# Row maxima of 112 pairs of key blocks found as s0 + relu(s1 - s0) in the attention stage of a two-layer block

## The reference, cut to what matters

```
q = _apply_rope(q, cos, sin)
k = _apply_rope(k, cos, sin)
att = jnp.einsum('bhtd,bhsd->bhts', q, k) * scale
att = jnp.where(causal_mask[None, None], -jnp.inf, att)
att = jax.nn.softmax(att, axis=-1)
o = jnp.einsum('bhts,bhsd->bhtd', att, v)
```

## Time and profile before

| | us |
|---|---|
| median of 3 runs (1504.44 to 1509.45) | 1509.25 |
| the profiled execution, its own time | 1505.93 |
| its span, first to last instruction | 1504.2 |
| busy in the span: PE, DVE, ACT, POOL | 1316.1, 1276.6, 998.6, 321.6 |

### The profile page before, as it was taken

One profiled execution on the slowest core, in us unless ns is written; L12 is line 12 of the kernel. 1 busy time (PEld: TensorE's weight loads), 2 busy tenths in 40 slices (PEclk: granted clock), 3 DMA queues, 4 the chain that ended last, 5 costly groups with the idle time before them and its releaser, 6 DMA issues. The chain is left out here.

```text
span 1504.2 us, 27425 instructions
## 1 busy us (share of the span) xinstructions
PE 1316.1 (87%) x9558; PEld 597.4 (40%) x9558; DVE 1276.6 (85%) x2276; ACT 998.6 (66%) x1316; POOL 321.6 (21%) x574
## 2 busy tenths in 40 slices
PE   4786999999999999999999986999767767889987
PEld 2444223232232332323322212766533334467754
DVE  6896899999999999999999942799878999765668
ACT  3452365888888888888888896665357666356642
POOL 3220000110102111020110202333100077300475
PEclk9887688999999999999999998999968888899999
DMA  6887402141423304242043024596354155686776
GB/s 204 277 261 211 63 28 45 22 81 27 83 46 42 84 7 78 46 79 49 6 78 77 12 49 116 158 317 208 123 192 141 37 176 178 226 260 208 229 228 196
DMA packets 158521, 186.16 MB, mean 124 GB/s; under 512 B 18228, under 2 KB 134708, under 8 KB 157364
## 3 DMA queue, kind: packets, MB, share of 16 engines
q1 hardware_dynamic: 135384, 151.45, 37.5%
q0 software_dynamic: 6144, 16.79, 3.6%
q10 hardware_dynamic: 16864, 16.26, 3.1%
HBM read 100.81 MB, written 83.36 MB: 122 GB/s over the span
## 5 line engine op out<-in xcount | busy, mean ns | idle before, releaser
L1333 DVE TENSOR_REDUCE att_m_part<-att_mx 128x1 f32<-128x512 f32 (+3 forms) x1152 | 680.6, 653 | 30.3 <-PE att_mx L1401 13.5
L1363 ACT ACTIVATE att_prob<-att_score,late_score_scale 128x1024 f32<-128x1024 f32 (+3 forms) x640 | 594.9, 987 | 166.3 <-PE att_score L1440 164.1
L1401 PE MATMUL att_mx<-early_kop,early_qop 48*128 48x512 f16 (+3 forms) x1280 | 354.9, 367 | 23.0 <-DVE att_neg_m L1312 6.1
L1423 PE MATMUL att_pv<-att_prob,early_v 128*32 128x512 f32 (+3 forms) x2560 | 304.1, 547 | 2.1 <-POOL att_prob L1300 2.0
L1440 PE MATMUL att_score<-early_qop,early_kop 50*128 50x512 f16 (+3 forms) x1280 | 252.9, 356 | 11.1 <-ACT att_prob L1363 10.1
L1401 PEld LDWEIGHTS att_mx<-early_kop,early_qop 48*128 48x128 f16 x1280 | 98.5, 94 | 374.1 <-DVE att_m_part L1333 346.3
L1300 POOL TENSOR_SCALAR_AFFINE_SELECT att_prob<-att_prob 128x256 f32<-128x256 f32 x256 | 102.7, 406 | 669.7 <-ACT att_prob L1363 668.9
L2231 PE MATMUL rwkv_prod<-rwkv_xm,late_mixT 128*128 128x512 f32 x192 | 99.2, 672 | 34.5 <-ACT rwkv_kvr L2185 25.6
L1440 PEld LDWEIGHTS att_score<-early_qop,early_kop 50*128 50x128 f16 x1280 | 72.1, 94 | 71.7 <-ACT att_prob L1363 55.9
L2453 POOL DMA_INDIRECT moe_yg<-results,routing_slot_i x64 | 65.0, 1016 | 125.4 <-issue 124.3
L1980 POOL DMA_INDIRECT rows<-rwkv_xs,routing_slot_i x64 | 66.7, 1042 | 115.6 <-DVE routing_slot_i L2072 96.4
(11 more groups left out here) (263 smaller groups left out, 1759.7 us busy)
## 6 DMA issues: line engine op xcount, KB each, us to landing
va<-qkv_v SPq DMA_DIRECT2D x8, 1024.0 KB, 6.4
early_v<-va SPq DMA_DIRECT2D x8, 1024.0 KB, 6.8
routing_xp<-parts SPq DMA_DIRECT2D x32, 256.0 KB, 3.6
moe_xt<-rows SPq DMA_DIRECT2D x30, 256.0 KB, 3.2
rows<-att_zeros SPq DMA_DIRECT2D x8, 928.0 KB, 6.5
early_kop<-qk SPq DMA_DIRECT2D x48, 128.0 KB, 4.5
results<-moe_y ACTq DMA_DIRECT2D x24, 256.0 KB, 2.8
results<-blend_x ACTq DMA_DIRECT2D x22, 256.0 KB, 3.1
```

What stands on the lines that cost most here:

```text
L1333: nc.vector.tensor_reduce(cells[:, sides[0]:sides[-1] + 1, some], mx[:, banks[0]:banks[-1] + 1, 0:len(hps) * w].rearrange("p a (h w) -> p ...
L1363: nc.scalar.activation(prob[:, r % (PROBS * HP), :, n0:], score[:, r % 2, :, n0:], ACT.Exp, scale=late_weights.score_scale[:, 0:1])\
L1401: op = nc.tensor.matmul(bank[:, n * w:(n + 1) * w], qop[rows, slot, t, hp, i * P:(i + 1) * P], kop[rows, slot, hp, c * GT:c * GT + w], sta ...
L1423: op = nc.tensor.matmul(pv[at, n0:], v[:, slot, j, at], prob[:, (st * HP + h // 2) % (PROBS * HP), h % 2, n0:], start=(j == 0), stop=(j == ...
```

## The change

For 7 blocks of maxima, (iteration 0, t = 2) and (iterations 0 to 5, t = 3), the key blocks 0 and 1 are no longer two pieces. For each tile of 128 queries and head pair (8 in a block, 56 in all, each with two sides, so 112 pairs) the program now does this:

- POOL writes once for an iteration `k_minus` = -k for keys 0 to 511, in two instructions of 48x1024 f16 (L1337).
- PE computes s1 - s0 for both sides into a score bank: four matmuls of 512 columns in place of the two of key block 1 (`differences`, L1492).
- ACT takes the Relu of the 1024 columns into `over`, a ring of OVERS = 7 in SBUF (`overs`, L1432).
- PE computes s0 into an `att_mx` bank, as before, and DVE adds the two and takes the row maximum with `tensor_tensor_reduce` (L1389), in place of two `tensor_reduce`.

The score banks are now numbered by the place in the joint list of Relus and exponentials. The order of the pieces within a paired block changes (by tile and head pair, then key block), and `matrix_order` gets a fourth kind of work, "over", and other costs.

```diff
+    PAIRED = [(0, LATE - 1)] + [(it, LATE) for it in range(NIT - 2)]
+    OVERS, AHEAD = 7, 60
...
+        if in_pairs:
+            rest = [(i, (hp,), c) for i in range(TG) for hp in range(HP) for c in (0, *range(2, t + 1))
+                    if c < t or HP * width(t, i, t) > GT]
...
-        hand, back, mask, row, copy, soon = 250, 120, 420, 6500, 580, 200
-        turn = {"max": 0, "score": 1, "value": 2}
+        hand, back, mask, row, copy, soon, load = 250, 120, 420, 6500, 580, 200, 9000
+        turn = {"max": 0, "over": 1, "score": 2, "value": 3}
...
+                if it > 1:
+                    need.append(value_end[(it - 1) * NS - 1] + load if len(value_end) >= (it - 1) * NS else None)
+                if None not in need and (not paired(it, e) or pair_of[it, e] < done["over"]):
+                    ready.append((max(need) + back, "max"))
+            n = done["over"]
+            if n < total["over"] and done["max"] > max(pair_at[n] - AHEAD, place[0, ("turn", 0)]) and (n < OVERS or done["max"] > pair_end[n - OVERS]) \
+                    and done["score"] >= ((pairs[n][0] - 1) * NS + last_step[LATE - 1] + 1) * HP:
+                ready.append((max([0] + exp_end[-2:-1]) + back, "over"))
...
-                    dve = max(dve, pe + hand) + 70 + size * len(e[5]) * 100 // 96
+                    dve = max(dve, pe + hand) + 118 + size * len(e[5]) * 100 // 96
...
+            if kind == "over":
+                pe = when + 20 + GT * 5 // 6
+                start = max([act, pe + hand] + ([taken[pair_end[n - OVERS]] + hand] if n >= OVERS else []))
+                act = start + 894
...
-                act = start + 30 + columns(t, j) * 2 * 100 // 96
+                act = start + 380 + columns(t, j) * 2 * 593 // 1000
...
-                pe = when + 150 + columns(t, j) * 5 // 3
+                pe = when + 20 + columns(t, j) * 5 // 3
...
+        over = s.sb("over", [P, OVERS, 2, GT])
+        k_minus = s.sb("k_minus", [P, 2, HP, GT], F16)
...
+            def minus(it):
+                slot = it % 2
+                pool.wait_ge(first_in[slot], (it // 2 + 1) * FIRST)
+                if it > 1:
+                    last_pair = max(n for n, at in enumerate(pairs) if at[0] == it - 2)
+                    pool.wait_ge(score_done.sem, score_done.done(ring["over", last_pair]))
+                for a in range(2):
+                    rows = slice(HALF * a, HALF * a + ROWS)
+                    nc.gpsimd.tensor_scalar(k_minus[rows, slot], kop[rows, slot, :, 0:GT], -1.0, None, ALU.mult)\
+                        .then_inc(k_turned, 1)
+                    pool.wait_ge(k_turned, it * 2 + a + 1)
...
+                if paired(it, e):
+                    n, a = pair_of[it, e], sides[0]
+                    dve.wait_ge(exp_done.sem, exp_done.done(ring["over", n]))
+                    nc.vector.tensor_tensor_reduce(over[:, n % OVERS, a], mx[:, banks[0], 0:w], over[:, n % OVERS, a], 1.0,
+                                                   LOWEST, ALU.add, ALU.max, cells[:, a, some]).then_inc(m_found, 1)
+                    return
...
+            def overs(n):
+                at = ring["over", n]
+                if n >= OVERS:
+                    act.wait_ge(m_found, pair_end[n - OVERS] + 1)
+                act.wait_ge(score_done.sem, score_done.done(at))
+                nc.scalar.activation(over[:, n % OVERS], score[:, at % 2], ACT.Relu).then_inc(exp_done.sem, 1)
...
+            def differences(n):
+                it, t, i, (hp,) = pairs[n]
+                slot, at = it % 2, ring["over", n]
+                if n == 0 or pairs[n - 1][0] < it:
+                    pe.wait_ge(first_in[slot], (it // 2 + 1) * FIRST)
+                    pe.wait_ge(k_turned, it * 2 + 2)
+                    if it == 0:
+                        pe.wait_ge(att_in.third_in, att_in.THIRD)
+                pe.wait_ge(exp_done.sem, exp_done.freed(at, 2))
+                for step, moving in enumerate((kop[:, slot, hp, GT:2 * GT], k_minus[:, slot, hp])):
+                    for a in range(2):
+                        rows = slice(HALF * a, HALF * a + ROWS)
+                        op = nc.tensor.matmul(score[:, at % 2, a], qop[rows, slot, t, hp, i * P:(i + 1) * P], moving[rows],
+                                              start=step == 0, stop=step == 1)
+                op.then_inc(score_done.sem, 1)
```

More of the change, by code:

```diff
@@ new lines, in chunks, with paired, with_turn @@
+        return [("max", t, *item, (a,)) for item in whole + rest for a in range(2)]
+    def paired(it, e):
+        return e[0] == "max" and e[4] == 0 and (it, e[1]) in PAIRED
+    def with_turn(it, t):
+        own = [(it, e) for e in chunks(t, (it, t) in PAIRED)]
+        return own[:6] + [(it, ("turn", t - 1)) if t else (it - 1, ("turn", LATE))] + own[6:]
+    order_of = [(it, t) for it in range(NIT) for t in range(QB)]
+    entries = [at for n, (it, t) in enumerate(order_of) for at in with_turn(it, t) if at[0] >= 0]
@@ new lines, in attention_phase @@
+    entries.append((NIT - 1, ("turn", LATE)))
+    place = {entry: k for k, entry in enumerate(entries)}
+    pairs = []
+    for it, e in entries:
+        if paired(it, e) and (it, *e[1:4]) not in pairs:
+            pairs.append((it, *e[1:4]))
+    pair_of = {(it, e): pairs.index((it, *e[1:4])) for it, e in entries if paired(it, e)}
+    pair_at = [place[it, ("max", t, i, hps, 0, (0,))] for it, t, i, hps in pairs]
+    pair_end = [place[it, ("max", t, i, hps, 0, (1,))] for it, t, i, hps in pairs]
@@ L1105, in matrix_order @@
         exp_end, prob_end, value_end, out_end, found, rows = [], [], [], [], {}, {}
-        bank_end, order, done = [0] * BANKS, [], {"max": 0, "score": 0, "value": 0}
-        total = {"max": len(entries), "score": len(score_at), "value": len(value_at)}
+        over_end, taken = [], {}
+        bank_end, order, done = [0] * BANKS, [], {"max": 0, "over": 0, "score": 0, "value": 0}
+        total = {"max": len(entries), "over": len(pairs), "score": len(score_at), "value": len(value_at)}
         while done != total:
@@ L1118, in matrix_order @@
                 if (it, steps[st][0]) in rows and n // HP < done["value"] + PROBS:
-                    need = [rows[it, steps[st][0]]] + [end + back for end in exp_end[n - 2:n - 1] if n >= 2]
+                    need = [rows[it, steps[st][0]]] + [end + back for end in exp_end[-2:-1]]
                     ready.append((max(need), "score"))
@@ L1168, in attention_phase @@
     order = matrix_order()
+    through = [at for at in order if at[0] in ("over", "score")]
+    ring = {at: r for r, at in enumerate(through)}
     with ExitStack() as ctx:
@@ L1450, in _ @@
                     entry(*at)
+                elif kind == "over":
+                    differences(*at)
                 elif kind == "score":
```

54 lines of the change are left out of this document (30 added, 24 removed).

## The result

| | before | after |
|---|---|---|
| median, us | 1509.01 (1504.44 to 1509.45) | **1594.49** (1588.13 to 1599.26, 4 runs) |
| ratio | | **1.0576** [1.0555, 1.0596] |
| span of the profiled execution, us | 1504.2 | 1586.4 |
| mean granted clock of PE | 0.937 | 0.906 |

The account below looks back on a forecast made before the run. DVE was taken to set the 91.1 us attention iteration, with PE a few per cent behind. 38 us kept less 15 at the start gave 1505.9 - 23 = 1482.9, plus 3.3, stated as 1484 us; range 1462 to 1515.

Parts of the forecast that it names:

- DVE's work: Attention stage: 224 reduces (139.3 us) replaced by 112 pairs at 0.72 us (80.6 us), saving 58.7 us on DVE.
- scan-like rival: DVE's new instruction runs slower than an element a cycle, 1.36 us a pair, giving 1534 us; chance 0.07.
- ACT's work: Attention stage: 56 added Relus of 1024 columns at 0.96 us, 54 us in all, 7.7 for an iteration.
- The start: Behind block 0's turn, PE and DVE stall for `third_in`: 10.0 us, plus 5 at the low clock, 15 in all.
- DVE sets the period of an iteration, PE is a few per cent behind it: Attention stage: DVE is the bound of the 91.1 us iteration, with PE filled to 88 to 96%.
- new period of 86.3: Iterations 1 to 5 shorten from 91.1 to 86.3 us, keeping 4.8 of 8.4 each, 24 us in all.
- What costs nothing: POOL's negations and SP's work add no time; the planner's new costs favour no side, 5 us either way.
- SP issues nothing new: DMA issue by SP: the change adds nothing there, so no cost was counted.
- The new costs in the planner, 5 us either way: Changed planner costs alter the order elsewhere, favouring no side seen; 5 us either way put on it.
- Kept, iteration 0: In iteration 0, with ACT only 68% busy, 14 of the 16.8 us saved on DVE in two blocks are kept.
- PE or ACT takes over at the old period: Rival: Relus delay exponentials and value products, iterations stay at 91 us, giving 1507 us, no change; chance 0.14.
- The pairs interlock: Rival: late Relus in PE's and DVE's fixed order lengthen iterations 1 to 5 to 95 us, giving 1527; chance 0.05.

Follow-up runs that it names:

- e_start: Changed kernel with the first differences placed 18 matrix products later: 1596.56 us, ratio 1.0591 to the kernel before.
- b_half: Kernel before, with the 224 reduces that the change would pair reading only half of their columns, order unchanged: 1495.43 us, ratio 0.9901.
- e_all: Changed kernel, new planner costs kept, with earlier negation, planner's load 23 us, first differences 18 products later, no V wait at the maxima: 1511.29 us, ratio 1.0024.
- e_kminus: Changed kernel with POOL's negation before the masks of block 2 instead of behind them: 1561.38 us, ratio 1.0363 to before.
- e_load: Changed kernel with the planner's load cost raised from 9 to 23 us: 1564.19 us, ratio 1.0372 to before.
- f_old: Changed kernel, pairs kept, with the planner's three old costs: 1681.10 us, ratio 1.1154 to before.
- f_first: Changed kernel, pairs in iteration 0 only, old planner costs, earlier negation, load 23 us, first differences later, no V wait at maxima: 1497.60 us, ratio 0.9931.
- n_half_plan: Kernel before with 224 half-width reduces, planner told of them, planner's load 23 us, no V wait at maxima: 1564.19 us on a slower chip, ratio 0.9863.

## Why the prediction was wrong, step by step

- **DVE's work: right, though the close match of the sum is partly luck.** The main instruction takes 685 ns and the second 82, but from a pair to the next instruction in a row it is 0.61 us, not my 0.72; the reduces in a row stand 0.60 apart, so the second instruction is nearly hidden. All instructions of L1389 together keep DVE busy 73.6 us where I had 80.6. The 672 remaining reduces cost 425.1 / 672 = 0.633 us apiece instead of 0.622, 7 us more, since fewer stand close behind one another. The two cancel: 58.5 us saved against 58.7. The scan-like rival is out. The rule of the Trainium skill that I had weighed (Vector Engine (DVE) Microarchitecture Reference, Points that are easy to get wrong) is about two sources in SBUF, and no run here shows that case with an accumulator; with one source in PSUM nothing is halved, 685 ns for 512 elements against the reduce's 683. With the other statement of the Trainium skill (VectorE: DVE Perf Modes, Two Vector instructions with no wait between them), that an instruction that also writes its accumulator is two, the trace agrees: 112 reads of an accumulator stand behind 112 instructions.
- **ACT's work: right** in size, 1026 ns a Relu, 0.90 to 0.92 in a row (0.96 forecast), 48.3 us more in all (54 forecast).
- **The start: right.** PE stood 11.3 us for the DMA into `early_qop`, clock 0.50; I had said 10.0 from 152 us on. From 190 to 200 us the granted clock is 0.50, where it was 1.00 before. But e_start showed that the stall costs after nothing: without it the program waits as long further back.
- **"DVE sets the period of an iteration, PE is a few per cent behind it": the step that failed at the root.** I read DVE's 96% as a bound because its reduces stood behind one another, and PE's 88 to 96% as slack of 4 to 12%. b_half measures what DVE gives back when nothing else changes: 1.1 us of 91, or 1.2%. The new period of 86.3 in the sum (24 us kept in iterations 1 to 5) could not last; what lasts is 90 to 92. I had PE's own sum, 2.2 to 2.4 us in a step of 2.49, and took its lower end as a reason for slack.
- **"What costs nothing": three entries, all wrong, and the larger part of the miss.** Of the 110 us between 1484 and 1594, the four edits of e_all take back 83; the other 27, from 1484 to 1511, belong to the step above. (1) POOL's negations: 2.77 us each, against "about 2", and I judged their cover by the distance of POOL's masks. The cover that counts is PE's: its order has the first difference right where POOL starts. Taking the 5.6 us out of PE's way was worth 33 us (e_kminus). (2) "SP issues nothing new": true, but the load of the next iteration but one had 21 us to spare before (V landed at 494.7, needed at about 516). The new order gives the maxima a growing lead over the values, from 57 to 103 us; the load can only start when old values are done, and PE was sent to wait for it. 30 us (e_load). I never asked what a DVE that runs ahead would meet. (3) "The new costs in the planner, 5 us either way": 44 us by themselves without pairs, through the lower clock between iterations, and with them 87 us the other way (f_old against after).
- **Kept, iteration 0: right.** I kept 14 us there and took 15 off for the start. The last `att_neg_m` of block 3 comes at 233.7 us in after, 234.4 before, and at 222.2 in e_start, where the start doesn't stall: 12 us earlier. How much of this is DVE and how much the clock is open, as for f_first.
- **The rivals.** "PE or ACT takes over at the old period" had the true mechanism, with a chance of 0.14, and e_all is its time (1511 against its 1507). "The pairs interlock" named PE's fixed order as the danger, but by late Relus, and DVE waited under 1 us for those; the two waits that decided, for POOL and for a load, were in no rival.
- **A slip in the sum.** 1482.9 + 3.3 is 1486.2, 1.5% below the median shown, not 1484 and 1.7%. It changes nothing in the outcome.

The stalls of after add up to 24.1 + 31.6 + 2.5 + 11.3 = 69.5 us; four edits took back 83. The clock (0.906, against 0.937 in e_all as before) is what makes the rest likely: behind a stall PE runs at its lower level, with 0.42 us from one matmul to the next instead of 0.22, as at 448.5. By the granted clock PE spends about 175 us of the attention stage there in after, 62 before and 55 in e_all, part of it inside the stalls. How the 83 divides between stalls, clock and order was not measured.

**Open:** whether any order of this program gets under 89 us an iteration, and whether PE alone or PE with ACT holds it there. Every order tried came from the same planner; a hand-made one was not tried. Nor was a different split of pairs between iterations, beyond all and the first.

## To carry to other kernels

Before you pay to unload the busiest engine, make it faster for nothing, by letting it read half its data, and look at what comes through: b_half would have told in one run that 8 us saved are worth 1.1. When a change lets one part of a fixed order run ahead of another, list what had time to spare between the two, loads into shared slots first, and check each from the waiting engine's side. Costs in a planner are part of the change: run them alone. And before an order is blamed for a longer period, multiply the period by the granted clock of the same stretch: the new costs made the program 44 us longer here and left that product as it was.

## What was unexpected in the hardware's numbers

- The read of DVE's accumulator, a second instruction of 82 ns, costs almost nothing in a row: 0.61 us from one pair to the next instruction, 0.60 from one reduce to the next.
- POOL takes 2765 ns for a multiplication of 48x1024 fp16 values in SBUF, against 503 for 128x256 from fp32: 2.7 and 1.97 ns for an element of a partition. Scaling by free size from the nearest row gave 2.0 us, 27% too little; the two differ in type and in partitions as well.
- One chip ran the kernel before in 1583.23 us where the others took 1508 to 1509. In n_half_plan's trace, from that chip, the attention stage ends at 904 us, in b_half's at 908: the extra time lies behind the stage. The windows of the same 190 us show part of it, b_half first:

```profile
1110.00:1300.00 190.00, 136.66 (x538) 72.60 (x535) 163.38 (x237) 118.32 (x169) 74.18 (x80) 0.87 0.44 145
```
```profile
1110.00:1300.00 190.00, 115.27 (x399) 57.59 (x397) 132.07 (x177) 103.85 (x149) 65.33 (x64) 0.78 0.34 113
```

Every engine does less there; 37.5 us are one wait of DVE at L2215, whose end the profile puts down to "remote". What it waits for was not looked into, and only ratios on one chip are used above.
